# Four-row sums and their softmax taken off TensorE for 24 of 32 token tiles

## The reference, cut to what matters

```python
x = L0_attn_hidden_states                      # (4, 1024, 512)
xn = _layernorm(x, axis=-1)
# inside the attention part, with hidden_states = xn, RATIO = 4, C = 256
w_log = (hidden_states @ Wcmp + bcmp).reshape(Bq, C, RATIO)
w_cmp = softmax(w_log, axis=-1)                # four weights that sum to 1
entries = einsum('bcr,bcrh->bch', w_cmp, hidden_states.reshape(Bq, C, RATIO, HID))
ck = apply_rope(rmsnorm(entries @ Wk + bk, kn_w), block_ends)
cv = entries @ Wv + bv
# ... q, local keys and values, top-8 of q.ck, local window of 256, output product
x = x + attn(xn) + ffn(xn, input2)             # ffn: 8-bit casts of both sides, one product
```

## Time and profile before

| | |
|---|---|
| median of 3 runs | 2492.65 us (2492.36 to 2493.54) |
| span of the profiled execution, first to last instruction | 2492.2 us |
| mean granted TensorE clock | 1.000 |
| busy share PE, DVE, ACT, POOL | 99%, 80%, 67%, 70% |

### The profile page before, as it was taken

One profiled execution on the slowest core, in us unless ns is written; L12 is line 12 of the kernel. 1 busy time (PEld: TensorE's weight loads), 2 busy tenths in 40 slices (PEclk: granted clock), 3 DMA queues, 4 the chain that ended last, 5 costly groups with the idle time before them and its releaser, 6 DMA issues. The chain is left out here.

```text
span 2492.2 us, 56206 instructions
## 1 busy us (share of the span) xinstructions
PE 2462.4 (99%) x15574; PEld 2190.6 (88%) x15606; DVE 1996.7 (80%) x6637; ACT 1675.3 (67%) x4866; POOL 1749.7 (70%) x3150
## 2 busy tenths in 40 slices
PE   7999999999999999999999999999999999999998
PEld 6888888888888988888888889888888888888887
DVE  7788888888778887787777888887878878888786
ACT  5667777767666677667666666767676666666665
POOL 6787787776786666666677766666667767676674
PEclk9999999999999999999999999999999999999999
DMA  5433233333332122121441221221235213212301
GB/s 159 136 107 113 71 109 115 117 109 117 123 119 82 52 90 90 60 90 43 151 150 53 81 82 60 90 86 64 78 124 166 94 59 100 75 61 94 98 10 52
DMA packets 183530, 232.36 MB, mean 93 GB/s; under 512 B 19762, under 2 KB 101172, under 8 KB 183220
## 3 DMA queue, kind: packets, MB, share of 16 engines
q1 hardware_dynamic: 182644, 228.50, 28.3%
q10 hardware_dynamic: 576, 0.26, 0.1%
HBM read 162.64 MB, written 65.01 MB: 91 GB/s over the span
## 5 line engine op out<-in xcount | busy, mean ns | idle before, releaser
L1598 POOL TENSOR_TENSOR t<-raw,tB 128x128 f32<-128x128 f32 x512 | 226.4, 464 | 593.8 <-DVE raw L1167 593.7
L987 ACT ACTIVATE ch<-bVC,blT 128x128 fp32r<-128x128 f32 x512 | 160.5, 365 | 511.1 <-PE bVC L726 511.1
L631 PE MATMUL bQK<-wh,xh 128*128 128x512 f32 x1024 | 424.4, 414 | 0.0
L632 PE MATMUL bQK<-wl,xh 128*128 128x512 f32 x1024 | 403.8, 394 | 0.0
L633 PE MATMUL bQK<-wh,xl 128*128 128x512 f32 x1024 | 401.4, 392 | 0.0
L1542 POOL TENSOR_TENSOR r<-ss,mh 128x4 f32<-128x4 f32 x256 | 286.4, 1119 | 60.1 <-DVE ss L1175 57.5
L647 PE MATMUL bVC<-wh,xh 128*128 128x256 f32 x1024 | 310.0, 303 | 0.0
L954 ACT ACTIVATE P<-P,nm,r 128x256 f32<-128x256 f32 (+1 forms) x512 | 295.3, 583 | 0.0
L1203 DVE CUSTOM_DVE_ANT_0 P<-bS,cst 128x256 f32<-128x256 f32 (+1 forms) x512 | 204.2, 399 | 110.5 <-PE bS L679 106.1
L649 PE MATMUL bVC<-wh,xl 128*128 128x256 f32 x1024 | 289.4, 283 | 0.0
L648 PE MATMUL bVC<-wl,xh 128*128 128x256 f32 x1024 | 289.0, 282 | 0.0
(11 more groups left out here) (188 smaller groups left out, 7617.9 us busy)
## 6 DMA issues: line engine op xcount, KB each, us to landing
wh<-kept SPq DMA_DIRECT2D x144, 256.0 KB, 4.1
wl<-kept SPq DMA_DIRECT2D x144, 256.0 KB, 4.6
kept<-wh SPq DMA_DIRECT2D x48, 256.0 KB, 3.2
kept<-wl SPq DMA_DIRECT2D x48, 256.0 KB, 3.4
woh<-kepto SPq DMA_DIRECT2D x48, 256.0 KB, 3.2
wol<-kepto SPq DMA_DIRECT2D x48, 256.0 KB, 3.7
ini<-in_hidden_states SPq DMA_DIRECT2D x24, 256.0 KB, 4.5
xs<-xsh SPq DMA_DIRECT2D x24, 256.0 KB, 2.5
```

What stands on the lines that cost most here:

```text
L631: e.matmul(bQK[:, :], a, b, start=kt == 0, stop=False)
L632: e.matmul(bQK[:, :], a, bl, start=False, stop=False)
L1598: last = e.tensor_tensor(t2[:, :, :, d_], raw[:, u % 2, :, :, s_], tB[:, :, u % 8, d_].unsqueeze(1).broadcast_to([128, 2, 2, 32]), ALU.mult)
```

## The change: what it does

For tiles 8 to 31 (`FIRST_TILES` = 8) the softmax of four and the sum of four rows no longer use PE:

- `spread` (SP): the 128 logits, one per partition, go to DRAM; `gather` brings them back as 32 partitions of four. DVE takes the largest and subtracts it (`below_max`), ACT takes the exponentials with their sum (`exp_4`), DVE divides (`shares`); `give` writes the 128 weights to DRAM and `widen` reads them as one row of 128 for every partition, into `dg`.
- `whole_x` (POOL) adds the halves `xsh` and `xsl` to the tile in transposed form, `xf`; `weigh` (POOL) multiplies it with the row of weights; `fold` (POOL) adds neighbours in two instructions, 256 sums and then 128, the second into `et`.
- Removed for these tiles: `diagonal`, `exp_w`, `put_et` on ACT, `logits` and `entries` on PE, `group_max` and `weights4` on DVE.
- Each of the stages has a step of its own by `LAGS`. Tiles 16 to 31 begin four steps sooner (9 becomes 5 in `tile_base`), their blocks' `kv`, `put` and `rope` run 10 steps behind the last tile instead of 7, `turn`, `hi` and `lo` 12 instead of 9.
- The 8-bit product moves: `ffn_base(t)` is now the base of the next tile, so it meets that tile's `turn`, and the two are interleaved (`turn_ffn`), at the place of `turn` ahead of the scores. This again holds for 14 tiles.
- `xt` has three buffers instead of four; some semaphores are merged; `double` and the second `new_ck` of a sequence run one step later.

```diff
-    return t - AHEAD if t < 8 else 14 + 6 * (t - 8) if t < 16 else 64 * (t // 8 - 1) + 9 + 7 * (t % 8)
+    return t - AHEAD if t < 8 else 14 + 6 * (t - 8) if t < 16 else 64 * (t // 8 - 1) + 5 + 7 * (t % 8)
...
-        "max": (2, 2, 3), "ew": (3, 3, 4), "wm": (3, 3, 4), "et": (3, 4, 8), "park": (3, 3, 4)}
-BLOCK_LAGS = {"kv": (4, 5, 7), "put": (4, 5, 7), "rope": (4, 5, 7), "turn": (6, 6, 9), "hi": (6, 6, 9), "lo": (6, 6, 9)}
+        "max": (2, 2, None), "ew": (3, 3, None), "wm": (3, 3, None), "et": (3, 4, None), "park": (None, None, 4),
+        "spread": (None, None, 2), "gather": (None, None, 3), "below": (None, None, 4), "share": (None, None, 5),
+        "give": (None, None, 6), "widen": (None, None, 7), "whole": (None, None, 5), "weigh": (None, None, 8),
+        "fold": (None, None, 9)}
+BLOCK_LAGS = {"kv": (4, 5, 10), "put": (4, 5, 10), "rope": (4, 5, 10), "turn": (6, 6, 12), "hi": (6, 6, 12), "lo": (6, 6, 12)}
...
-    return 64 * (NB - 1) + 2 + 7 * t // 2 if t < NL else tile_base(t) + 5
+    if t < NL:
+        return 64 * (NB - 1) + 2 + 7 * t // 2
+    return tile_base(t) + 6 if t % 8 == 7 else tile_base(t + 1)
...
+            def spread(t):
+                e.wait_ge(S["wl"], t + 1)
+                e.dma_start(spread_l[t].rearrange("(p a) -> p a", a=1), smt[:, t % 2, 2:3]).then_inc(S["d_g0"], 16)
...
+                e.dma_start(l4, spread_l[t].rearrange("(g r) -> g r", r=4)).then_inc(S["d_g1"], 16)
...
+                e.dma_start(spread_w[t].rearrange("(g r) -> g r", r=4), w4).then_inc(S["d_g2"], 16)
...
+                e.dma_start(wide[:, :], bc(spread_w[t], 128)).then_inc(S["d_g3"], 16)
...
+            def turn_ffn(t, f):
+
+                e.wait_ge(S["xn"], t + 1)
                 e.wait_ge(S[free["T"][0]], free["T"][1])
                 e.wait_ge(S["q8"], 4 + ffn_pos(f) + 1)
                 e.wait_ge(S[free["Y"][0]], free["Y"][1])
                 for kt in range(KT):
                     c = slice(kt * 128, (kt + 1) * 128)
-                    m = e.matmul(entries_of(t)[:, kt * 32:(kt + 1) * 32], xt[:, t % XR, c], wm[:, :], start=True, stop=True)
+                    m = e.transpose(bT[:, c], xt[:, t % XR, c], ident)
                     if kt == KT - 1:
-                        m.then_inc(S["et"], 1)
+                        m.then_inc(S["xt"], 1)
                     last = e.matmul(bY[:, :], q8[:, ffn_pos(f) % QR, c], w2q[:, kt, :], start=kt == 0, stop=kt == KT - 1)
                 last.then_inc(S["ff"], 1)
...
+            def whole_x(t):
+                e.wait_ge(S["lo_x"], t + 1)
+                e.tensor_tensor(xf[:, :, :], f32(xsh[:, :, :]), f32(xsl[:, :, :]), ALU.add).then_inc(S["xf"], 1)
+
+            def weigh(t):
+                n = t - FIRST_TILES
+                e.wait_ge(S["xf"], 3 * n + 1)
+                e.wait_ge(S["d_g3"], 16 * (n + 1))
+                w = wide[:, :].unsqueeze(1).broadcast_to([128, KT, 128])
+                e.tensor_tensor(xf[:, :, :], xf[:, :, :], w, ALU.mult).then_inc(S["xf"], 1)
+
+            def fold(t):
+                n = t - FIRST_TILES
+                x4 = pair(xf[:, :, :]).rearrange("p (c r) -> p c r", r=4)
+                e.wait_ge(S["xf"], 3 * n + 2)
+                e.tensor_tensor(x4[:, :, 0:2], x4[:, :, 0:2], x4[:, :, 2:4], ALU.add).then_inc(S["xf"], 1)
+                e.wait_ge(S["xf"], 3 * n + 3)
+                e.wait_ge(S["kv"], t // 4)
+                x2 = xf[:, :, :].rearrange("p k (c r) -> p k c r", r=4)
+                e.tensor_tensor(et[:, :, (t % 4) * 32:(t % 4 + 1) * 32], x2[:, :, :, 0], x2[:, :, :, 1],
+                                ALU.add).then_inc(S["put_et"], 1)
```

More of the change, by code:

```diff
@@ L841, in run_tensor @@
                     fill(8)
-                if tile_at(s, "turn") is not None:
+                beside = tile_at(s, "turn") is not None and ffn_at(s, 3) is not None
+                if beside:
+                    turn_ffn(tile_at(s, "turn"), ffn_at(s, 3))
+                elif tile_at(s, "turn") is not None:
                     turn_x(tile_at(s, "turn"))
@@ L859, in run_tensor @@
                     values(u4, 1)
-                if tile_at(s, "turn") is not None:
-                    logits(tile_at(s, "turn"))
+                if tile_at(s, "max") is not None:
+                    logits(tile_at(s, "max"))
                 if u0 is not None:
@@ L1127, in run_scalar @@
                         hi_wo(q)
-                if tile_at(s, "norm") is not None:
+                if tile_at(s, "norm") is not None and tile_at(s, "norm") < FIRST_TILES:
                     diagonal(tile_at(s, "norm"))
@@ L1705, in run_gpsimd @@
                     power_x(tile_at(s, "power"))
+                if tile_at(s, "whole") is not None:
+                    whole_x(tile_at(s, "whole"))
+                if tile_at(s, "weigh") is not None:
+                    weigh(tile_at(s, "weigh"))
+                if tile_at(s, "fold") is not None:
+                    fold(tile_at(s, "fold"))
                 if s >= 0:
```

147 lines of the change are left out of this document (99 added, 48 removed), and 4 rows, old and new, of the table SIGNALS.

## The result

The changed kernel takes 2546.0 us (median of 4 runs, 2544.3 to 2552.8), before takes 2493.1 (4 runs, 2492.4 to 2493.7). The ratio is 1.0217, with a 95% interval of 1.0205 to 1.0229. I had predicted 2485, with a range of 2472 to 2496: the run came out 53 us slower than before, where I had forecast 7.5 faster.

A forecast was written before the change was run, and what follows sets the result against it. The prediction took PE's instruction stream to bound the kernel. Gains of 24.0 us less losses of 9.0, 2.8, 4.2 and 0.5 left 7.5 us off the 2492.2 us span, so a median of 2485, range 2472 to 2496.

The forecast's parts named there:

- Costed at nothing: Small transfers, late weights, ACT and DVE savings, three `xt` buffers and SP's queue order: all claimed to cost or gain nothing.
- `ckv` of the odd blocks: PE waits for POOL's `fold` in blocks 3, 5 and 7: 3.6 + 2.7 + 2.7 = 9.0 us, from 6.5 to 13.
- The waits of `turn_ffn`: PE wants `q8` earlier in 14 steps: 0.2 us each, 2.8 us in all, between 0 and 11.
- my 4.2 for `tr` and `out_proj`: In the 14 `turn_ffn` steps PE waits for `lo_x` and `init`: 0.3 us each, 4.2 us, 0 to 8.
- The overlap: Product beside a turn hides part of the weight loads: 0.1 us in 14 tiles, 1.4 us, between 0 and 2.8.
- The gains: Leaving PE's stream: logits 5.3, entries alone 8.1, entries beside the product 7.6, overlap 1.4, bank bY 1.6; sum 24.0 us.
- the 1.6 of the bank bY: PE's second waits, at `out_proj` in nine turns, go: 2.7 us less 1.1 of longer `lo_x` waits, net 1.6 us.
- POOL's rows: `whole_x`, `weigh` and `fold` add 3.8 us a tile, 91 us in 24 tiles, covered by POOL's idle time except at `ckv`.
- under the 2.4 us of idle time: POOL's new work, at most 1.3 us in a step, was claimed to fit its mean idle time per step.
- 0.5 beside the `ckv` waits: Cost to PE of POOL rows holding DVE up, for turns of tiles 8 to 15 where `weigh` precedes the scores: 0.5 us.
- The rivals: Alternatives to the forecast (0.46): waits hidden, 2474 to 2479 (0.20); all handed back, 2489 to 2495 (0.21); slower, 2503 (0.13).
- The third: Slower: POOL rows hold DVE's `nm`, 76 us of DVE delay, a third reaching PE, giving 2503 us; chance 0.13.

The follow-up runs named there:

- run 1: Changed kernel with the four Wo loads issued ahead of the four small transfers in SP's step; 2516.6 us, ratio 1.0095.
- run 10: Changed kernel with run 1's and run 2's edits, `turn_ffn`'s product a step behind the turn, and `spread` issued at the end of ScalarE's step; 2503.6 us.
- Run 6: Kernel before with an unused transfer of 128 4-byte pieces added straight ahead of the Wo loads in six steps; 2543.7 us, ratio 1.0201.
- run 2: Changed kernel with the last tile of each batch begun one step earlier, its block's product staying in place; 2534.3 us.
- run 11: Changed kernel with run 1's and run 2's edits, `turn_ffn`'s product a step behind the turn, and `whole_x`, `weigh`, `fold` on 4 columns; 2494.4 us.
- Run 16: run 13 with GpSimd's `quant_nan` of tiles 16 to 30 moved behind the normalising of its step; 2487.4 us, ratio 0.9976.
- run 12: Changed kernel with run 1's and run 2's edits, `turn_ffn`'s product a step behind the turn, and `spread` sending one constant row; 2494.7 us, ratio 1.0004.
- run 9: Changed kernel with `spread` sending the same 512 bytes as one row of a constant tile, leaving out the logits; 2535.8 us.
- run 13: Changed kernel with run 1's and run 2's edits, `turn_ffn`'s product a step behind the turn, and the small-transfer chain of tiles 19 and 27 two steps later; 2496.7 us.

## Why the prediction was wrong, point by point

**The step that failed** is in "Costed at nothing": "SP passes its queue in order, and its new waits are for work one step old, so loads behind them stay early". In step 85 the work one step old, `normalise`, ended 4.5 us into the step, and the Wo loads behind that wait have only 0.9 us to spare in before (the last landed at 843.15, asked for at 844.09). I never looked at which load had the least room. The runs put 29 us on this order (run 1), by the late issue (4.3 us in step 85) and by the pieces' hold (7.5 more).

**The bound that was left out.** I wrote that no row shows transfers of 4 bytes per partition, and then priced them at nothing but their own lateness. The four-byte write takes 7.8 us to land in the median (run 10), and what is in flight with it waits. Run 6 shows that this alone can cost 50 us.

**`ckv` of the odd blocks.** Right in place, number and length: POOL in step 127 and PE behind it, where I had 1254.35 and a wait of 2.7 us:
```profile
1280.77 0.41 POOL L1728 TENSOR_TENSOR et<-xf 128x128 f32<-128x128 f32 x1
```
```profile
1281.23 3.61 PE L841 MATMUL bY<-wkv,et 128*128 128x256 f32 x8 [2.23 <-POOL et L1728]
```
The waits are 2.8, 2.2 and 2.2 us, 7.3 against my 9.0. What was short is the price, the wait and no more ("the wait is lost in full"): the row itself shows 3.61 us for eight products at half clock, a cost of which the prediction has nothing. By run 2 the three cost 11.7 us.

**The waits of `turn_ffn`.** Mis-sized: 12.2 us for `q8` and `acc` against 2.8. Beyond the work and the listed waits the 14 steps lose 4.5 us, a size near my 4.2 for `tr` and `out_proj`; but no wait of `tr` for `lo_x` is listed in them (the two in the list are those of steps 29 and 53), so the agreement may be luck. The overlap, 1.4 us in my sum, is 0 in steps 86 and 150, the two without a wait.

**The gains.** Eight tiles (8 to 15) at 0.22 + 0.81 us and the 1.6 of the bank bY are 9.8 us; 6.7 - 2.6 = 4.1 stood in hand at step 66, and run 11, without GpSimd's new work, has 7.0 in hand there. So most of it is there once that work is gone, and the work took some 3 us of it; what the rest went into isn't shown. For the tiles beside the product, turn and product alone make 7 x (0.44 + 0.87) = 9.2 us a batch, and 12.0 with my waits (0.2 + 0.3) and my overlap (0.1). Run 16 reaches 10.9, run 12 stands at 15.6, and after at 18.8, its stall for Wo in step 93 included. The price of a turn was taken in step 111, where no `quant_nan` stands ahead of `r`; the new bases of tile and product put the two together, for every tile beside the product, which I took from the diff as a change of place alone.

**POOL's rows.** Priced well: 3.6 us a tile for my 3.8, and the strided ones shorter than their bounds:
```profile
L1718 POOL TENSOR_TENSOR xf<-xf,dg 128x512 f32<-128x512 f32 x24 | 31.8, 1325 | 0.0
L1711 POOL TENSOR_TENSOR xf<-xsh,xsl 128x512 f32<-128x512 f32 x24 | 30.8, 1283 | 0.0
...
L1724 POOL TENSOR_TENSOR xf<-xf 128x256 f32<-128x256 f32 x24 | 14.7, 613 | 0.0
L1728 POOL TENSOR_TENSOR et<-xf 128x128 f32<-128x128 f32 x24 | 10.0, 416 | 1.9
```
But "under the 2.4 us of idle time" is a mean, and room on GpSimd doesn't cover what its rows do to `nm` and to the factors behind them. By run 11 this work costs 9 us, where my sum has 0.5 beside the `ckv` waits.

**The rivals.** The third had the sign, which is luck: its mechanism is real but small. It asked for 76 us on `nm`, and `nm` is 8.9 us longer in all; it shows in steps 29 and 53, where `weigh` holds `nm`, at 1.0 us each. No rival was about the DMA queue, and none about the clock.

What stays open: why a piece of 4 bytes holds what one of 64 doesn't. 128 pieces of 16 bytes were not tried, so the bound lies between 4 bytes and 64 for 128 pieces. The size of a piece wasn't parted from its place either: in DRAM the 4-byte pieces lie side by side in 512 bytes, those of 64 in 8 KB. Which of GpSimd's three operations costs the 9 us, and how much of it is shared access, wasn't parted.

## What to carry to other kernels

Before new transfers or waits go into a queue, find the load in that queue with the least room between landing and use, and put it first; here loads with 0.9 us of room decided 29 us. A transfer of single 4-byte values from 128 partitions is no small thing: price it by what it delays, keep it clear of loads that are due, or send longer pieces (here 16 or 64 bytes). And a moved step is priced by the engines' order in the step that it moves into, not by the step that it leaves.

## What the hardware showed that I had not expected

- 128 writes of 4 bytes from SBUF to DRAM: 7.1 to 9.6 us from issue to landing (run 10), and 7.4 to 9.3 until `gather` behind it could go (the 20 tiles of after in which SP stood idle for it); other transfers of the same queue issued up to 4 us behind take 10.2 to 11.9 us in the median instead of 3.7, and one issued 0.5 us ahead 9.9. The same 512 bytes as a row, as 32 pieces of 16 bytes, or 8 KB as 128 pieces of 64: no time (ratios 1.0001, 1.0003, 0.9999), though what follows the pieces of 16 lands 0.9 us later than behind the row.
- The TensorE clock fell to half after waits of 2.2 to 2.8 us too, for 3.4 to 10.2 us, but not each time: not after 2.8 us in step 66 of runs 1 and 9, nor after 2.3 in step 101 of run 10. Runs 12, 13 and 16, without such stretches but for the last microseconds of 13 and 16, show 1.000 in the mean.
- A VectorE instruction on four elements took 1.1 us for 0.16 when a GpSimd row of 1.3 us had begun 0.2 us ahead of it (steps 29 and 53 of the changed kernel).
